# A cross-attention and expert kernel on one core: no flush of units at a batch's end, tokens from the residual sum, norm weights folded, diagonals by DMA

## The reference

```python
# attention (mLSTM cell), per batch: q = layernorm(x), k = v = ctx, 8 heads of 32
log_f = log_sigmoid(fg);  cs = cumsum(log_f)
log_D = where(causal, cs[:, :, None] - cs[:, None, :], -inf) + ig[:, None, :]
C = (q @ k.T / sqrt(32)) * exp(log_D - max(log_D))
h = (C / (max(|C.sum|, exp(-max_log_D)) + 1e-6)) @ v
x = x + layernorm(h) * ln_scale
# experts: u = layernorm(x)
xn = u * rsqrt(mean(u * u) + eps) * g           # g_shared or g_routed
expert(u) = gelu(xn @ W1 + b1) @ W2 + b2        # W1 256 x 1024, W2 1024 x 256
scores = sigmoid(u @ centroids)                 # 8 routed experts, the best 2 are taken
out = x + u + sum of 2 shared experts + sum of gates * 2 routed experts
```

## Time and profile before

| | us |
|---|---|
| median of 3 runs | 1440.33 |
| profiled execution | 1436.01 |
| its span, first to last instruction | 1434.3 |
| TensorE busy | 1170.9 (82%) |
| VectorE busy | 1026.1 (72%) |
| ScalarE busy | 793.5 (55%) |
| GpSimd busy | 389.5 (27%) |

### The profile page before, as it was taken

The page is one execution under the profiler, slowest core; times in us unless marked ns, Lnnn a source line. Parts: engine busy times, 40 slices in busy tenths (PEclk is TensorE's granted clock), DMA queues, the critical chain, the costliest instruction groups (busy, mean ns, idle before and its releaser), DMA issues. The chain is left out here.

```text
span 1434.3 us, 22326 instructions
## 1 busy us (share of the span) xinstructions
PE 1170.9 (82%) x7861; PEld 1008.2 (70%) x7861; DVE 1026.1 (72%) x2507; ACT 793.5 (55%) x1454; POOL 389.5 (27%) x397
## 2 busy tenths in 40 slices
PE   0363698797897987997978988599999999999996
PEld 0142477576676666775766777589888999899886
DVE  2356659568567676595684654588898889888984
ACT  2101355444553554554544443488888887888785
POOL 2312122041041121221410201144334433443343
PEclk9986799999999999999999998799999999999998
DMA  4899910000010010000000000677777777777772
GB/s 125 220 265 273 288 61 30 30 30 30 30 59 30 20 41 30 30 31 30 30 15 15 31 19 27 213 206 194 194 218 210 198 190 214 216 198 194 205 220 24
DMA packets 172563, 168.08 MB, mean 117 GB/s; under 512 B 48362, under 2 KB 159860, under 8 KB 172452
## 3 DMA queue, kind: packets, MB, share of 16 engines
q1 hardware_dynamic: 120884, 109.43, 25.3%
q10 hardware_dynamic: 37264, 38.54, 10.5%
q0 software_dynamic: 14304, 18.69, 6.3%
HBM read 109.42 MB, written 57.22 MB: 116 GB/s over the span
## 5 line engine op out<-in xcount | busy, mean ns | idle before, releaser
L1233 DVE TENSOR_TENSOR wlo<-raw,whi 128x512 fp32r<-128x512 f32 x312 | 228.2, 732 | 35.1 <-ACT whi L1184 31.4
L1155 PE MATMUL bank<-xhi,whi 128*128 128x256 f32 x624 | 178.8, 287 | 25.5 <-issue 20.2
L1206 ACT ACTIVATE hraw<-bank,b 128x256 f32<-128x256 f32 x312 | 148.2, 475 | 86.2 <-PE bank L1155 53.1
L1273 DVE TENSOR_TENSOR hlo<-hraw,hhi 128x256 fp32r<-128x256 f32 x312 | 183.1, 587 | 17.5 <-ACT hhi L1209 5.7
L973 PE MATMUL bank<-whs,shared_hhi 128*128 128x256 f32 x512 | 150.0, 293 | 50.1 <-DVE shared_hlo L727 50.1
L1135 PE MATMUL bank<-whi,hhi 128*128 128x256 f32 x624 | 180.3, 289 | 12.8 <-issue 11.4
L523 ACT ACTIVATE shared_hraw<-bank,b1s 128x512 f32<-128x512 f32 x128 | 88.1, 688 | 180.8 <-PE bank L988 171.4
L1155 PE MATMUL bank<-xlo,whi 128*128 128x256 f32 x624 | 175.3, 281 | 0.0
L1155 PE MATMUL bank<-xhi,wlo 128*128 128x256 f32 x624 | 175.1, 281 | 0.0
L1135 PE MATMUL bank<-whi,hlo 128*128 128x256 f32 x624 | 173.4, 278 | 0.0
L1135 PE MATMUL bank<-wlo,hhi 128*128 128x256 f32 x624 | 173.3, 278 | 0.0
(11 more groups left out here) (248 smaller groups left out, 2834.7 us busy)
## 6 DMA issues: line engine op xcount, KB each, us to landing
raw<-in_L_ffn_W_r_dram SPq DMA_DIRECT2D x78, 1024.0 KB, 7.8
sorted_tokens<-base ACTq DMA_DIRECT2D x1, 33540.0 KB, 137.6
xt<-sorted_tokens SPq DMA_DIRECT2D x39, 260.0 KB
big<-in_L_ffn_W_s_dram SPq DMA_DIRECT2D x4, 1024.0 KB
xb<-in_x_dram SPq DMA_DIRECT2D x8, 512.0 KB, 4.6
cb<-in_ctx_dram SPq DMA_DIRECT2D x8, 512.0 KB, 3.6
xr<-in_x_dram SPq DMA_DIRECT2D x8, 512.0 KB, 3.6
out_dram<-base ACTq DMA_DIRECT2D x8, 512.0 KB, 2.9
```

What stands on the lines that cost most here:

```text
L1155: last = nc.tensor.matmul(ub[:, 0:T], w[i][:, wsl], x_[i][:, k, :], start=k == 0 and t == 0, stop=k == KD - 1 and t == 2)
L1206: nc.scalar.activation(hraw[:, m % NHB, :], psum[m % NU][:, 0:T], ACT.Gelu, bias=b1[i][:, m:m + 1]).then_inc(t_gelu, 1)
L1233: nc.vector.tensor_tensor(wlo[i][:, psl], raw[i][:, psl], whi[i][:, psl].bitcast(fp32), ALU.subtract).then_inc(t_wlo, 1)
L1273: nc.vector.tensor_tensor(hlo[:, m % NHB, :], hraw[:, m % NHB, :], hhi[:, m % NHB, :].bitcast(fp32), ALU.subtract).then_inc(t_hlo, 1)
```

## The change

What it does, edit by edit:

1. The down-projections of a batch's last two units move into units 0 and 1 of the next batch; only the last batch flushes. The buffers `hraw`, `hhi`, `hlo` are counted through over the batches. `finish(b - 1)` comes behind unit 1 of batch b, and the first down-projection of batch b waits for it.
2. The variance of the residual sum gives both roots in one Newton iteration on a tile `roots` of twice the width: one for the layer norm, one for layer norm and RMS norm together. `un` comes straight from `x1`; `hh` is formed two steps later.
3. g_shared is multiplied into the shared up weights in setup. The hand-over loses its VectorE product, and ScalarE's rounding waits for `unT` itself.
4. The rows of `exp_rhs` on the diagonals are written by eight DMAs on SP from `low16`, which VectorE now forms with the minus sign. The selection product goes. The exponent matmuls wait for these DMAs. SP's loads are put in another order around them.
5. `ORDER` is new: the front has nine steps, all named F, instead of six, and they stand elsewhere.

The diff, without the lines that only rename a buffer index (`k % NHB` to `h` or `n`) and the closing yields of the generators:

```diff
@@ -117,6 +117,7 @@
+        roots = A("roots", [P, 5, 2, J])
@@ -299,14 +300,21 @@
-                    nc.vector.tensor_tensor(wls[:, e, :], big[e][:, :], whs[:, e, :].bitcast(fp32), ALU.subtract
-                                            ).then_inc(s_wls, 1)
+                    for k in range(KD):
+                        ksl = slice(k * HID, (k + 1) * HID)
+                        nc.vector.scalar_tensor_tensor(wls[:, e, ksl], big[e][:, ksl], gs_col[:, k:k + 1],
+                                                       whs[:, e, ksl].bitcast(fp32), ALU.mult, ALU.subtract)
+                    nc.vector.tensor_tensor(wls[:, e, WN:2 * WN], big[e][:, WN:2 * WN],
+                                            whs[:, e, WN:2 * WN].bitcast(fp32), ALU.subtract).then_inc(s_wls, 1)
...
-                    nc.scalar.copy(whs[:, e, :], big[e][:, :]).then_inc(s_whs, 1)
+                    for k in range(KD):
+                        ksl = slice(k * HID, (k + 1) * HID)
+                        nc.scalar.activation(whs[:, e, ksl], big[e][:, ksl], ACT.Copy, scale=gs_col[:, k:k + 1])
+                    nc.scalar.copy(whs[:, e, WN:2 * WN], big[e][:, WN:2 * WN]).then_inc(s_whs, 1)
@@ -341,17 +349,17 @@
-        ORDER = "S 0 H 0 U A 1 U F 1 U Q 2 U F 2 B U P 3 U 3 D U G T E U T U T U R V U V U V U R U W U X C U".split()
+        ORDER = ("S 0 H 0 U A 1 U F 1 U Q 2 U F 2 B U P 3 U 3 D F U T E U T U F T U V U U W V F U X F U F U F F U").split()
@@ -365,6 +373,8 @@
+                        if b > 0 and k == LAG - 1:
+                            parts["finish"](b - 1)
@@ -375,13 +385,11 @@
-                elif step in "FGRC":
+                elif step == "F":
...
-            if units:
-                parts["finish"](b)
@@ -392,6 +400,7 @@
+            parts["finish"](B - 1)
@@ -412,18 +421,30 @@
+                def diagonals(b):
+                    sp.wait_ge(lhs_ready, b + 1)
+                    if b > 0:
+                        sp.wait_ge(exp_done, J * b)
+                    for h in range(NH):
+                        sp.dma_start(exp_rhs[h:HR:NH, :, h, :], low16[h:HR:NH, :].rearrange("p (j s) -> p j s", s=P)
+                                     ).then_inc(s_diag, 16)
...
-                for b in range(1, B):
-                    sp.wait_ge(q_ready, b)
-                    load(xb, x_v, b, s_x)
-                    sp.wait_ge(state_done, b)
-                    load(cb, c_v, b, s_c)
-                    sp.wait_ge(x1_ready, b)
-                    load(xr, x_v, b, s_xr)
+                for b in range(B):
+                    if b > 0:
+                        sp.wait_ge(state_done, b)
+                        load(cb, c_v, b, s_c)
+                    if b + 1 < B:
+                        sp.wait_ge(q_ready, b + 1)
+                        load(xb, x_v, b + 1, s_x)
+                    if b > 0:
+                        sp.wait_ge(x1_ready, b)
+                        load(xr, x_v, b, s_xr)
+                    diagonals(b)
@@ -515,15 +539,17 @@
-                    if k >= NHB:
+                    h = (U * b + k) % NHB
+                    if U * b + k >= NHB:
@@ -546,7 +572,9 @@
-                    sc.wait_ge(xraw_ready, b + 1)
+                    sc.wait_ge(unT_ready, b + 1)
+                    if b > 0:
+                        sc.wait_ge(up_done, U * b)
@@ -566,15 +594,18 @@
+                def newton(own, square, product, v, root):
+
+                    own.done(ts(root.bitcast(i32), v.bitcast(i32), -0.5, float(0x5F3759DF), ALU.mult, ALU.add))
+                    for _ in range(3):
+                        own.done(tt(square, root, root, ALU.mult))
+                        own.done(stt(product, square, -0.5, v, ALU.mult, ALU.mult))
+                        own.done(stt(root, product, 1.5, root, ALU.add, ALU.mult))
@@ -630,17 +662,15 @@
-                    own.done(nc.vector.tensor_copy(low16[0:HR, :], rest[0:HR, 1, :]))
-                    low = low16[0:HR, :].rearrange("p (j s) -> p j s", s=P)
-                    for h in range(NH):
-                        last = ts(exp_rhs[0:HR, :, h, :], low, negsel[:, h:h + 1], None, ALU.mult)
-                    last.then_inc(lhs_ready, 1)
+                    ts(low16[0:HR, :], rest[0:HR, 1, :], -1.0, None, ALU.mult).then_inc(lhs_ready, 1)
@@ -699,20 +729,20 @@
-                    rsqrt(own, mv[:, :, 1], LN_EPS, nw)
-                    yield
-                    own.done(normed(hh, x1, mv, nw))
-                    own.done(tt(nw[:, 0, :], nw[:, 3, :], nw[:, 3, :], ALU.mult))
-                    own.done(tt(nw[:, 4, :], nw[:, 0, :], mv[:, :, 1], ALU.mult))
-                    rsqrt(own, nw[:, 4, :], RMS_EPS, nw)
-                    yield
+                    ts(roots[:, 2, 0, :], mv[:, :, 1], LN_EPS, None, ALU.add)
+                    own.done(ts(roots[:, 2, 1, :], mv[:, :, 1], 1.0 + RMS_EPS, LN_EPS * RMS_EPS, ALU.mult, ALU.add))
+                    newton(own, *(roots[:, n, :, :].rearrange("p r j -> p (r j)") for n in range(4)))
...
-                        last = ts(un[:, j, :], hh[:, j, :], nw[:, 3, j:j + 1], None, ALU.mult)
+                        last = ts(un[:, j, :], x1[:, j, :], mv[:, j, 0:1], roots[:, 3, 1, j:j + 1], ALU.subtract, ALU.mult)
                     last.then_inc(un_ready, 1)
-                    own.done(nc.vector.reciprocal(nw[:, 4, :], nw[:, 3, :]))
-                    yield
+                    yield
+                    yield
+                    for j in range(J):
+                        ts(hh[:, j, :], x1[:, j, :], mv[:, j, 0:1], roots[:, 3, 0, j:j + 1], ALU.subtract, ALU.mult)
+                    own.done(nc.vector.reciprocal(roots[:, 4, 0, :], roots[:, 3, 1, :]))
+                    own.done(tt(nw[:, 4, :], roots[:, 4, 0, :], roots[:, 3, 0, :], ALU.mult))
@@ -737,11 +767,6 @@
-                    dve.wait_ge(unT_ready, b + 1)
-                    dve.wait_ge(logit_done, b + 1)
-                    for k in range(KD):
-                        last = ts(unT[:, k, :], unT[:, k, :], gs_col[:, k:k + 1], None, ALU.mult)
-                    last.then_inc(xraw_ready, 1)
@@ -913,6 +941,7 @@
+                    pe.wait_ge(s_diag, 16 * NH * (b + 1))
@@ -966,12 +996,14 @@
-                    e, m = k // M, k % M
+                    if k == 0 and b > 0:
+                        pe.wait_ge(fin_ready, b)
+                    e, m, n = k // M, k % M, (U * b + k) % NHB
@@ -979,7 +1011,7 @@
-                    if k >= 2:
+                    if U * b + k >= 2:
@@ -988,9 +1020,9 @@
-                    if k >= LAG:
-                        second(b, k - LAG)
-                    if k == U - 1:
+                    if U * b + k >= LAG:
+                        second(*divmod(U * b + k - LAG, U))
+                    if U * b + k == U * B - 1:
```

More of the change, by code:

```diff
@@ L343, in xattn_moe_kernel @@
         unT_done, unT_ready, logit_done, logit_read = (sem(n) for n in ("unT_done", "unT_ready", "logit_done", "logit_read"))
-        xraw_ready, xhs_ready, xls_ready = (sem(n) for n in ("xraw_ready", "xhs_ready", "xls_ready"))
+        xhs_ready, xls_ready = sem("xhs_ready"), sem("xls_ready")
         base_ready = sem("base_ready")
@@ L509, in back @@
                         yield
-                    for _ in range(6):
+                    for _ in range(4):
                         yield
@@ L517, in back @@
                     yield
+                    yield
                 def unit(b, k):
                     sc.wait_ge(up_done, U * b + k + 1)
-                    if k >= NHB:
+                    h = (U * b + k) % NHB
+                    if U * b + k >= NHB:
                         sc.wait_ge(unit_done, U * b + k - NHB + 1)
-                    nc.scalar.activation(hraw[:, k % NHB, :], up_bank[k % 2][:, :], ACT.Gelu,
+                    nc.scalar.activation(hraw[:, h, :], up_bank[k % 2][:, :], ACT.Gelu,
                                          bias=b1s[:, k // M, k % M:k % M + 1]).then_inc(gelu_done, 1)
                     sc.wait_ge(gelu_done, U * b + k + 1)
-                    nc.scalar.copy(hhi[:, k % NHB, :], hraw[:, k % NHB, :]).then_inc(hhi_ready, 1)
+                    nc.scalar.copy(hhi[:, h, :], hraw[:, h, :]).then_inc(hhi_ready, 1)
                 def finish(b):
@@ L567, in moments @@
                     own.done(last)
+                def newton(own, square, product, v, root):
[4 more added lines that the diff above has]
+                        own.done(stt(root, product, 1.5, root, ALU.add, ALU.mult))
                 def rsqrt(own, v, e, nw):
                     own.done(ts(nw[:, 2, :], v, e, None, ALU.add))
-                    own.done(ts(nw[:, 3, :].bitcast(i32), nw[:, 2, :].bitcast(i32), -0.5, float(0x5F3759DF),
-                                ALU.mult, ALU.add))
-                    for _ in range(3):
-                        own.done(tt(nw[:, 0, :], nw[:, 3, :], nw[:, 3, :], ALU.mult))
-                        own.done(stt(nw[:, 1, :], nw[:, 0, :], -0.5, nw[:, 2, :], ALU.mult, ALU.mult))
```

(6 more changed lines are left out.)

9 lines of the change are left out of this document (6 added, 3 removed).

## The result

The changed kernel takes **1503.05 us** (median of 4, 1501.59 to 1506.46), the kernel before beside it 1439.15 (1435.84 to 1440.91): ratio **1.0443** [1.0425, 1.0460], slower by 64 us. Forecast were 1427 and 1406 to 1443. The experiments ran on other occasions, beside the kernel before at 1433 to 1435; so they are compared by their ratios to it, and 0.01 is then 14.3 us.

What follows compares the result with a forecast made beforehand. TensorE was taken as the bound, its idling as what can be won. Six passes -10.8, then -1.5 + 2.25 - 4.2 - 2.4 + 3.7 gave -13 us: from the median of 1440.33 to 1427, range 1406 to 1443.

Steps and rivals of the forecast that it cites:

- No flush, folded weights: Batch end and hand-over: the 5.12 wait goes, the 2.25 wait is covered, the scaling by gs_col (0.87) goes.
- Diagonals: Before block 0's exponent matmuls: DMAs land 4.9 us after the low parts (3.9 to 7.4); TensorE waits 3.2.
- setup and first pass together: Setup +0.7 for more split instructions, shorter last chain and earlier hand-over in the first pass: together -1.5 (-3 to +4).
- Query transposes: Moved ahead of unit 6: they wait for head block 3's sums, covered only by 0.36 of transposes: +1.7.
- Tokens: Before the token transposes: TensorE idles about 4.1 us for VectorE's tokens.
- the 1.1 and 1.15 ahead of it: TensorE's idling: 1.1 as unit 11's up matmuls wait for ScalarE, 1.15 for the split of unit 9.
- The chain through step 4: Gates before unit 9: VectorE waits for ScalarE's logarithm (67.4) before x1 is formed; tokens are done at 77.5.
- GpSimd ahead of the state matmuls: At the pass's end: TensorE waits 1.35 for GpSimd's weighted values; next state matmuls start at 93.95, not 98.9.
- The clock: Behind the waits for tokens and diagonals, 12 occasions: one or two falls, about 2.5 each, +3.7 in all.
- My own rival: Clock falls after the tokens' and the diagonals' waits in each pass: ten more falls, +25, 1452; chance 0.10.
- The last two passes: Seventh pass -4.2 in waits and -2.4 by the clock; last pass +2.8 for two more down-projections.
- slower: Chances by clock 0.10, late diagonals 0.06, a flush that stays 0.04; as some end within 2.9 us, 0.14.

Runs made afterwards that it cites:

- experiment 2: The changed kernel with 30 matmuls of 512 bf16 columns more ahead of TensorE's wait for the diagonals; 1472.12 us, 1.0281.
- experiment 1: The changed kernel with VectorE writing the eight diagonals again, with no DMAs and no wait for one; 1452.25 us, 1.0133.
- experiment 6: The kernel of experiment 1 with one of each batch's eight indirect scatters issued, the other seven tokens' rows left out; 1422.84 us, 0.9908.
- experiments 7 and 11: 7: kernel of experiment 5 with the front's gates and logarithm later, 1401.82 us; 11: on 7, further order changes with earlier diagonals and hand-over, 1375.71 us.
- experiment 12: The second kernel of experiments 7 and 11, with the residual's first step directly behind the down-projection and gates and logarithm behind x1's moments; 1358.85 us, 0.9481.
- experiment 5: The kernel of experiment 1 with the query transposes again behind the unit that follows the down-projection, as before the change; 1421.65 us, 0.9922.

## Why the prediction was wrong

The forecast was -13 us, the profiled execution grew by 65.6. Of the miss of 79, 21.5 lie before the first hand-over (-1.5 forecast, +20.0 measured), 52 in the six passes and 5 in the last two.

- **No flush, folded weights: right.** The waits of 5.12, 2.25 and 1.04 went; together -2.5%.
- **Diagonals: the term that failed most.** I put the last landing 4.9 us behind low16, near the low end of 3.9 to 7.4, from an issue of 0.27 and the landing of 1 KB. Measured 7.2: 8 x 0.75 for the issues, 1.2 behind them. The mechanism and the bound were right, the choice between the ends was not: the nearest row was a load from DRAM, and none had a copy within SBUF.
- **The same DMAs where nothing stands beside them: a term that I left out.** For setup and first pass together I forecast -1.5; it was +20.0, of which 2.9 are setup's spread. Two bare waits of 7.40 and 6.94 replace copies that nothing waited for, and the clock behind them costs 2.4 each (experiment 2). Without the DMAs it is -1.6 (experiment 1).
- **Query transposes: 1.7 forecast, 3.37 measured: a releaser that I overlooked.** I let them wait for head block 3's sums, which ended at 305.70. They wait for ScalarE's copy of the gates as well, which ended at 306.75 in that pass, beneath unit 6, so the same trace gives about 2.6. The copy starts 2.5 to 3.3 us behind the gate transposes in the passes of before and 3.24 in the pass after; the scatters run beside it in both kernels, and with one scatter it is 0.64 (experiment 6). Timeline of ScalarE, before and after:

```profile
306.17 0.58 ACT L539 COPY frow<-bank 8x512 f32<-8x512 f32 x1 [4.55 <-remote]
```

```profile
444.63 0.58 ACT L565 COPY frow<-bank 8x512 f32<-8x512 f32 x1 [5.36 <-remote]
```

- **Tokens: 4.1 forecast, 3.75 measured, with the 1.1 and 1.15 ahead of it at 0.81 and 1.08.** The chain through step 4 was read rightly.
- **GpSimd ahead of the state matmuls: 1.35 forecast, none.** Its product took 4.02 us for the 5.14 of the earlier trace rows, in a stretch in which VectorE no longer worked beside it for most of the time. TensorE came to the exponents the earlier, and the diagonals took it.
- **The clock: one or two falls forecast in all, three in the pass shown** (0.63, 0.57, 0.65), worth 2.4, 1.6 and 1.4. The first is measured by experiment 2, the two others are their length times the missing share. Behind the diagonals the clock fell in all eight places, behind the tokens in all six passes, behind the query transposes in five of six. My own rival named the falls at the tokens and the diagonals, and I gave it 0.10; its time of 1452 us was still 51 too low. The Trainium skill (TensorE: Matmul & The Clock Gate, HAM oscillation) has the rule that I cited, that a loop's idle gaps throttle TensorE anew each time; this trace agrees for the first two waits, and for the third in five passes of six.
- **The last two passes: -3.8 forecast, +1.1 measured.** The waits in them were right (3.73 for 3.9 at the tokens, 2.21 for 2.4 at the hand-over); 2.00 us stand at the last batch's first down-projection, which now waits for the reading of the sums. I had put that at nothing, or 1.3 if its cover went.

From the exponents of one pass to the next state matmuls are 95.5 us for the forecast 89.6: 2.4 + 1.7 + 1.6 + 1.4 - 1.35, less 0.7 at the tokens and the two waits ahead of them, give 5.05 of the 5.9; 0.8 stay open. With 2.8 for the diagonals' landing (10.3 behind the start of the state matmuls, forecast 7.55) that is 105.8 for 97.15.

Two sums of the prediction don't come out. The waits named for the seventh pass give -3.8, not -4.2 (3.9 + 2.4 - 2.25 - 3.3 - 4.51). And where slower falls from 0.20 to 0.14, since some of it can't be told from none, the 0.06 belong to the same time (0.18), and faster stays at 0.68. Neither changes why it failed.

## What to carry to other kernels

Before an engine's work is given to DMAs, count the issues one behind the other at a measured price of the same kind of DMA, and place them where independent work stands, in the pipeline's filling too. When a long wait is taken away, look at what it covered. A chain gets no shorter because TensorE's work is moved away from it: the wait is set by the chain, and TensorE just arrives earlier (experiments 7 and 11); shortening the chain took it away (experiment 12). And before a step is moved up to a wait that was covered, list every signal that its code waits for, not the one that seems last.

## What the runs showed of the hardware

- A 3 KB copy within SBUF, 3 partitions by 512 bf16 in rows of 128, holds SP's or ScalarE's queue for 0.75 us; a 512 KB load 0.42.
- A small DMA behind 33.5 MB on the same engine's queue: four took 98.9 us to issue.
- Eight indirect scatters on GpSimd, against one, delay the start of waiting work by 1.5 us on VectorE and 2.5 on ScalarE (experiment 6).
- VectorE and GpSimd slow each other: the product took 4.02, 5.15 and 6.30 us, casts of 24x512 0.42 or 0.73, by whether and for how long they ran side by side. The Trainium skill (SBUF — State Buffer, SBUF: two separate sides) speaks of an exclusive lock for a whole instruction on a shared pair of ports; the traces agree that both lose, and don't show the lock.
- The length of a wait alone does not tell whether the lower clock follows. In the changed kernel the query transposes behind 3.37 us ran at 0.57 in the pass shown (0.66 us for the first two) and at full clock a pass earlier:

```profile
341.08 0.41 PE L907 MATMUL bank<-ident,qn 128*128 128x128 f32 x2 [3.37 <-issue]
```

- Likewise behind waits of 2.42 us at the exponents, twice in the kernel of experiment 5:

```profile
251.57 0.39 PE L955 MATMUL bank<-causal,identb 128*128 128x512 bf16 x1 [2.42 <-DVE big L674]
...
346.85 0.61 PE L955 MATMUL bank<-causal,identb 128*128 128x512 bf16 x1 [2.42 <-DVE big L674]
```
